# Ten states summed in five chains of three instead of eight in four, with a new timetable, in a Mamba block on one core

## The reference

```python
h = _layernorm(x) * (1 + ca) + sa
x_ssm, z = split(h @ w_in.T + b_in)                  # 512 + 512
dt = softplus(x_ssm @ w_dt.T + b_dt)
Bm = x_ssm @ w_B.T + b_B ; Cm = x_ssm @ w_C.T + b_C  # 16 states each
# scan over the 4096 positions, for each of 512 channels and 16 states
h = exp(A * dt) * h + dt * Bm * x_ssm
y = sum(h * Cm, axis=states)
y = (y + D * x_ssm) * silu(z)
x = x + ga * (layernorm(y @ w_out.T + b_out + residual) * gamma + beta)
h = _layernorm(x) * (1 + cb) + sb
x = x + gb * ffn(h)      # 512 -> 64, 16 relu units for each of the 64, 64 -> 512
```

## Time and profile before

| | before |
|---|---|
| median of 3 runs | 4281.64 us |
| the profiled execution | 4274.35 us |
| its span | 4272.6 us |
| TensorE busy | 4033.6 us, 94% |
| ScalarE busy | 3806.4 us, 89% |
| VectorE busy | 3646.4 us, 85% |
| GpSimd busy | 3460.0 us, 81% |

### The profile page before, as it was taken

The page is one execution under the profiler, slowest core; times in us unless marked ns, Lnnn a source line. Parts: engine busy times, 40 slices in busy tenths (PEclk is TensorE's granted clock), DMA queues, the critical chain, the costliest instruction groups (busy, mean ns, idle before and its releaser), DMA issues. The chain is left out here.

```text
span 4272.6 us, 68738 instructions
## 1 busy us (share of the span) xinstructions
PE 4033.6 (94%) x21664; PEld 2525.8 (59%) x21664; DVE 3646.4 (85%) x5134; ACT 3806.4 (89%) x6371; POOL 3460.0 (81%) x2058
## 2 busy tenths in 40 slices
...
GB/s 149 139 158 165 162 156 169 162 177 166 165 159 167 162 177 163 164 157 166 162 179 170 162 151 170 162 176 165 165 157 167 164 175 167 159 156 170 163 162 72
DMA packets 285535, 689.93 MB, mean 161 GB/s; under 512 B 31068, under 2 KB 33116, under 8 KB 285176
## 3 DMA queue, kind: packets, MB, share of 16 engines
q0 software_dynamic: 143360, 436.26, 56.0%
...
...
## 5 line engine op out<-in xcount | busy, mean ns | idle before, releaser
L415 POOL TENSOR_TENSOR work<-work,c_bc 128x1024 f32<-128x1024 f32 x1024 | 2614.4, 2625 | 327.1 <-DVE work L1221 144.4
L1221 DVE TENSOR_TENSOR_SCAN work<-work,state,b_ps 128x512 f32<-128x512 f32 x1792 | 2235.9, 1272 | 183.7 <-PE b_ps L528 158.1
L926 ACT ACTIVATE work<-u_td,b_td 128x512 f32<-128x512 f32 x2048 | 1455.7, 711 | 180.8 <-DVE u_td L1306 90.6
L916 ACT ACTIVATE work<-dt_t,neg_a 128x512 f32<-128x512 f32 x2048 | 1453.9, 710 | 23.9 <-DVE work L1221 23.9
L528 PE MATMUL b_ps<-ident,work 128*128 128x128 f32 x8192 | 1214.3, 277 | 113.6 <-DVE work L1221 69.1
L528 PEld LDWEIGHTS b_ps<-ident,work 128*128 128x128 f32 x8192 | 960.1, 142 | 596.9 <-issue 261.3
L426 POOL DMA_DIRECT2D work<-work x512 | 477.5, 933 | 237.6 <-DMA work<-work 118.2
L603 PE MATMUL y_ps<-ident,work 128*128 128x128 f32 x4096 | 558.7, 276 | 20.1 <-DMA work<-work 19.9
L603 PEld LDWEIGHTS y_ps<-ident,work 128*128 128x128 f32 x4096 | 470.2, 141 | 171.2 <-issue 120.1
L677 PE MATMUL dense<-w_out_t,proj 128*128 128x512 f32 x1024 | 515.8, 606 | 0.0
L735 PE MATMUL dense<-xs_t,w_dt_t 128*128 128x512 f32 x1024 | 495.8, 593 | 0.0
...
## 6 DMA issues: line engine op xcount, KB each, us to landing
work<-work POOLq DMA_DIRECT2D x512, 512.0 KB, 5.5
c_bc<-c_d SPq DMA_DIRECT2D x512, 256.0 KB, 3.6
xn<-in_x SPq DMA_DIRECT2D x128, 256.0 KB, 5.2
dt_t<-tmp POOLq DMA_DIRECT2D x64, 512.0 KB, 5.1
work<-xs_t POOLq DMA_DIRECT2D x64, 512.0 KB, 6.3
xsh_d<-par_d SPq DMA_DIRECT2D x32, 1024.0 KB, 13.2
xsh_d<-in_x POOLq DMA_DIRECT2D x32, 1024.0 KB, 8.6
x<-xsh_d POOLq DMA_DIRECT2D x64, 512.0 KB, 7.0
```

What stands on the lines that cost most here:

```text
L415: gp.tensor_tensor(made_here, both(hs, HS_RING, s * U + i), c_bc[:, (s * N + n) % C_RING:(s * N + n) % C_RING + 1, :].to_broadcast([P, 2, ...
L916: A(decay[:, (s * U + i) % DEC_RING, :], dt_t[:, s % 2, j, :], ACT.Exp, scale=neg_a[:, j, n:n + 1]).then_inc(S["dec_done"], 1)
L926: A(v[:, n % V_RING, tb, :], u_td[:, tb, :], ACT.Copy, scale=b_td[:, s % 2, tb, n:n + 1]).then_inc(S["v_done"], 1)
L1221: V.tensor_tensor_scan(hs[:, (s * U + i) % HS_RING, :], decay[:, (s * U + i) % DEC_RING, :], b_ps[:, i % 2, :], state[:, i:i + 1] if s % N ...
```

## The change

`HELD` gets states 12 and 13. A fifth chain 12+13+14 is summed by DMAs: four more of them in a step (20 in place of 16, and the two of the skip as before). TensorE adds states 2, 5, 8, 11, 14 and 15, so 24 units in a step in place of 32. The step size is still put together by two DMAs. All slots of the timetable are new; the lines that the prediction speaks of:

```diff
-    HELD = (0, 1, 3, 4, 6, 7, 9, 10)
+    HELD = (0, 1, 3, 4, 6, 7, 9, 10, 12, 13)
...
-        xs.2.2@36 xs.2.3@36 xs.3.0@36 xs.3.1@36 xs.3.2@37 xs.3.3@38 dt.0.0@38 dt.0.1@38 x2.0@40 dt.0.2@40
+        xs.2.1@38 xs.2.2@38 xs.2.3@39 xs.3.0@40 xs.3.1@40 xs.3.2@42 xs.3.3@43 dt.0.0@44 dt.0.1@45 x2.0@46
...
-        store=(5, 10, 13, 18),
+        store=(13, 13, 13, 18),
...
-        dt_add=(49, 52),
-        u_mul=(54, 54, 56, 56),
-        gate=(38, 62, 63, 10),
+        dt_add=(47, 51),
+        u_mul=(52, 53, 53, 54),
+        gate=(43, 57, 59, 8),
...
-        xn2=(37, 37, 37, 37),
+        xn2=(42, 42, 42, 42),
...
-        y_copy=(7, 7, 7, 7),
+        y_copy=(7, 8, 8, 8),
...
-        y=(15, 18, 18, 18, 31, 31, 32, 34, 40, 42, 42, 42, 50, 50, 51, 52, 54, 55, 55, 56, 56, 57, 58, 58, 62, 63, 63, 63, 63, 64, 68, 68),
-        sum=(5, 8, 9, 11, 13, 16, 17, 20, 23, 25, 30, 31, 36, 37, 42, 44, 45, 48),
-        spread=19,
-        x_add=63,
+        y=(17, 17, 20, 22, 30, 32, 33, 33, 40, 42, 44, 44, 52, 52, 55, 55, 69, 69, 70, 70, 70, 70, 70, 70),
+        sum=(5, 8, 10, 12, 13, 15, 18, 19, 23, 24, 30, 31, 33, 35, 44, 45, 46, 48, 56, 57, 60, 62),
+        spread=31,
+        x_add=38,
```

More of the change, by code:

```diff
@@ L48, in build_program @@
     AT = dict(
-        store=(5, 10, 13, 18),
-        c_store=54,
-        x1=(18, 26),
-        bout=57,
-        dt_add=(49, 52),
-        u_mul=(54, 54, 56, 56),
-        gate=(38, 62, 63, 10),
-        relu=(63, 63, 2, 2, 2, 2, 7, 8),
-        gm=9,
-        skip=(12, 12, 12, 15),
-        rstdx=20,
-        xn=(20, 20, 20, 20),
-        t2=(18, 20, 24, 25),
-        rstd2=37,
-        xn2=(37, 37, 37, 37),
-        h2=(40, 45, 47, 50),
-        h=(22, 25, 26, 28),
-        xs=(32, 34, 37, 38),
@@ L67, in build_program @@
-        cb=54,
-        bt=54,
-        edt=(46, 48, 50, 51),
-        ldt=(46, 48, 50, 51),
-        ez=(29, 59, 60, 10),
-        lz=(32, 59, 60, 10),
-        sig=(35, 59, 60, 10),
-        y_copy=(7, 7, 7, 7),
-        yz=(9, 10, 11, 13),
-        out=(14, 16, 17, 20),
-        pre=(15, 18, 20, 24),
-        dt=(43, 46, 49, 51),
-        ut=(60, 61, 62, 62),
-        z=(27, 59, 61, 63),
-        s=62,
-        stx=(9, 15, 16, 18),
-        nmrx=19,
-        st2=(29, 32, 36, 37),
-        nmr2=37,
```

49 lines of the change are left out of this document (40 added, 9 removed).

## The result

The changed kernel takes 4309.2 us, the median of 3 runs (4304.12 to 4311.33), against 4281.64. The ratio is 1.0073, with a 95% interval from 1.0058 to 1.0088. The forecast was 4228 us and faster; the time lies in the range given, on the other side of no change.

The account below looks back on a forecast made before the run. TensorE was taken to bound 112 of 128 us a step, VectorE with ScalarE the rest. Between -6.2 and +0.7 us a step it took -1.5, 48 us over 32 steps, giving a 4228 us median, range 4165 to 4320.

Parts of the forecast that it names:

- What bounds the kernel: The step cut in three: TensorE bounds 112 of 128 us (slots 8 to 63), VectorE with ScalarE the other 16.
- What is removed: Eight y_ps units a step off TensorE, 3.5 us; slots 40 to 63 lose 5.7 us and receive 5.2.
- What is added: Four summing DMAs a step, 4.9 us of GpSimd in slots 40 to 63, bringing it to 53.1 us there.
- The wait foreseen in slot 46: GpSimd's DMA of units 44 and 45 waits 0.9 us for that of units 40 and 41 to land.
- The wait foreseen at 3.3 us behind the spread in slot 31: GpSimd waits 3.3 us for a summing DMA landing late beside the 1 MB spread, moved from slot 19.
- The sum: Limits of the three stretches added up: -6.2 to +0.7 us a step, of which -1.5 was taken.
- The slow end: Each stretch held by its fullest engine, plus the same loss as before: 128.9 us a step, 0.7 slower.
- The burst of late y units: Six units on TensorE in slot 6, 2.6 us; VectorE's wait of some 1.2 us lies beside ScalarE's excess.
- DMAs get in each other's way: Rival: landings in slots 40 to 63 rise to 10 us, step some 3 us longer, 4378 us; chance 0.20.
- The burst of slots 5 and 6: Rival: this burst and ScalarE's fuller slots 0 to 7 outweigh the gain, about +1 us a step, 4314; chance 0.05.
- The clock: Rival: gaps in slots 8 to 63 bring TensorE's half clock there, twice a step, 4330 us; chance 0.02.
- No net gain: Rival: GpSimd and ScalarE fill what TensorE frees in slots 40 to 63, 4274 to 4288 us; chance 0.16.

Follow-up runs that it names:

- e6_old_left_out: The kernel before without the eight y units of states 12 and 13 in slots 54 to 58, left out of the sum: 4283.72 us, ratio 1.0026.
- e9_early_left_out: The kernel before without the eight y units of states 2 and 5 in slots 15 to 34, their DMAs kept: 4275.53 us, ratio 0.9990.
- e13: The kernel before with one ScalarE decay tile in eight made on 64 of 512 columns: 4281.59 us, ratio 0.9992.
- e15: The kernel before with two GpSimd products of 32 made on 64 of 512 columns: 4279.8 us, ratio 0.9989.
- e10_late_eight: The kernel before with only its last eight y units moved later, five into slots 1 to 5 of the next step: 4279.99 us, ratio 0.9998.
- e4: The kernel after with its four new summing DMAs a step moving 16 of 512 columns: 4291.54 us, ratio 1.0035 to before.
- e5: The kernel after without the fifth chain's four summing DMAs, states 12 and 13 left out of the sum: 4300.13 us, ratio 1.0055 to before.
- e7: The kernel after with the places of before for everything between slots 21 and 47: 4502.23 us, ratio 1.0529 to before.
- e17: The kernel after with slot 46's dt matmuls and turns spread over slots 45 to 51, followers moved later: 4490.09 us, ratio 1.0508 to before.
- e2: The kernel after with eight states held as before, y units of states 12 and 13 back in slots 55 to 58: 4343.58 us, ratio 1.0157 to before.
- e12: The kernel after without its eight late y units in slots 5 and 6, states 14 and 15 left out: 4268.71 us, ratio 0.9974 to before.

## Why the prediction was wrong

**What bounds the kernel: the step that failed.** "So TensorE bounds 112 of 128 us" took 60 of 61 and 50.9 of 51.2 us of busy time for a limit that is TensorE's alone. `e6_old_left_out` and `e9_early_left_out` took 3.5 us of full-clock work from it at two places inside those 112 and won nothing; `e13` to `e15` took 2.5 to 3.9 us a step from the other engines and won at most 0.2%. In slots 8 to 15 and 20 to 35 three engines are full together (the windows above), and the air that the long windows showed for ScalarE and VectorE stood in other slots than the work. That relieving two or three engines together would be given back there is argued from those windows; no run tried it. In slots 40 to 59 the windows give TensorE 2.0 us more than the next engine, and `e6` still won nothing; what holds that stretch is open.

**What is removed.** The count was right (1024 matmuls, 3.5 us a step at full clock), and its value was not 3.5 to 5.7 us: busy time fell by 68.3 / 32 = 2.1 us a step, and the rest of the span, in which TensorE stands still, grew from 239.0 to 342.9 us, 3.2 a step. Where TensorE was alone, slots 60 to 63, ScalarE's 13.56 us allow 2.5 at most, and `e10_late_eight` won 1.1 of it, only to lose it in slots 0 to 7. The stretch that I took as slots 0 to 7 in fact reached to about slot 10, so the fullness of VectorE at its start was read too mildly as well.

**What is added.** The wait foreseen in slot 46 is there, 0.9 us foreseen and 1.00 in this step:

```profile
2005.26 0.86 POOL L426 DMA_DIRECT2D work<-work  x1 [1.00 <-DMA work<-work]
```

GpSimd in slots 40 to 63 is busy 17.98 + 23.25 + 9.61 = 50.8 us, foreseen with its waits 53.1. The wait foreseen at 3.3 us behind the spread in slot 31 is 2.3 to 5.2 us in most steps, and 7.4 to 7.7 in steps 10, 17 and 24. The fifth chain's DMAs cost 0.2 to 0.4% (`e4`, `e5`), up to 0.5 us a step.

**The sum.** Its two ends were -6.2 and +0.7 us a step, from a least limit and from the fullest engine. The slow end, which takes each stretch by its fullest engine, was nearly right: +0.9 by the medians, +1.5 by the steps 4 to 29 of the trace. "Between the ends I take -1.5" gave weight to an end that ignored ScalarE and VectorE. That it was nearly right is in part luck: its terms are engines' busy times, and what lengthened the mean step is something else. The burst of late y units, priced at nothing ("It lies beside ScalarE's excess"), was measured at 1.2 us, most of it by the lower clock. The late landing of slot 33 makes slots 36 to 39 4.0 us longer in 3 of 26 steps, 0.5 on the mean. The `dt` burst of slot 46, of which I had counted the pairs but not their place, makes slots 44 to 47 5.7 us longer, but the two runs that took it apart (`e7`, `e17`) came out slower, so it has no price of its own.

**The rivals.** *DMAs get in each other's way* (0.20): not on the mean. Landings rose from 5.5 to 6.1 us on the median, 7.5 in slots 48 to 63, under the 8 from which it decides; the late landings of slot 33 are of its kind, but rare and not in slots 40 to 63. *The burst of slots 5 and 6* (0.05, 4314 us) came nearest, in place and time, but its companion, ScalarE's fuller slots, was not told apart. *The clock* (0.02) was put too low and in the wrong place: it is the larger part of that burst's 1.2 us, right where the late units stand, and costs little in the gaps behind, where it was looked for. *No net gain* (0.16) is what the steps at full clock show, 128.1 us against 128.2.

**By runs, in per cent of before.** New timetable with eight held +1.6 (`e2`), chain on it -0.8, together +0.7. Without the late units the kernel after is at -0.3 (`e12`), so these units are worth 1.0. What the new places of slots 20 to 23 and 52 to 59 cost was not told apart.
